# Moving one more of the four token blocks of each product by B from ScalarE to GpSimd in a fused selective-scan and mixture-of-experts kernel

## The reference, cut to what matters

```python
def _mamba_block(x, p):
    xn = _rmsnorm(x, p['norm_w'])
    xz = xn @ p['Win']
    xp, z = jnp.split(xz, 2, axis=-1)
    xc = jax.nn.silu(_causal_depthwise_conv(xp, p['conv_w'], p['conv_b']))
    dbc = xc @ p['Wx']
    dt, Bm, Cm = jnp.split(dbc, [DT_RANK, DT_RANK + D_STATE], axis=-1)
    delta = jax.nn.softplus(dt @ p['Wdt'] + p['bdt'])
    A = -jnp.exp(p['A_log'])
    y = _selective_scan(xc, delta, A, Bm, Cm, p['Dp'])
    y = y * jax.nn.silu(z)
    return x + y @ p['Wblk']
```

## Time and profile before

| | |
|---|---|
| median of 3 runs | 2395.76 us (2388.49 to 2397.93) |
| the profiled execution | 2392.5 us |
| its span, first to last instruction | 2390.7 us |
| first and last scan begin at | 67.5 and 1929.9 us |
| busy over the whole span | PE 1910.8, DVE 1957.4, ACT 1697.5, POOL 1414.9 us |
| busy in the first 1822.6 us after the first scan (67.5 to 1890.12) | PE 1415.4, DVE 1572.5, ACT 1488.2, POOL 1359.8 us |
| mean granted clock of TensorE | 0.934 |

### The profile page before, as it was taken

The page is one execution under the profiler, slowest core; times in us unless marked ns, Lnnn a source line. Parts: engine busy times, 40 slices in busy tenths (PEclk is TensorE's granted clock), DMA queues, the critical chain, the costliest instruction groups (busy, mean ns, idle before and its releaser), DMA issues. The chain is left out here.

```text
span 2390.7 us, 35098 instructions
## 1 busy us (share of the span) xinstructions
PE 1910.8 (80%) x10784; PEld 1200.9 (50%) x10784; DVE 1957.4 (82%) x1824; ACT 1697.5 (71%) x3050; POOL 1414.9 (59%) x1365
## 2 busy tenths in 40 slices
PE   5677777777777777777777777777778669999998
PEld 2344444444444444444444444444444348998998
DVE  3688888888888888888888888888888977776775
ACT  3787888788878888888888888888878723333333
POOL 2477777777777777777777777777777720000000
PEclk8789999999999999999999999999998879999999
DMA  7222222222222222222222222222222400000000
GB/s 225 70 57 70 59 73 59 68 56 73 58 73 57 70 55 70 55 70 55 70 55 70 56 70 58 72 58 72 58 69 58 127 1 10 10 10 10 9 5 10
DMA packets 81482, 139.49 MB, mean 58 GB/s; under 512 B 21264, under 2 KB 39312, under 8 KB 76816
## 3 DMA queue, kind: packets, MB, share of 16 engines
q1 hardware_dynamic: 75024, 120.36, 19.5%
q10 hardware_dynamic: 6400, 18.42, 2.5%
HBM read 63.85 MB, written 7.74 MB: 30 GB/s over the span
## 5 line engine op out<-in xcount | busy, mean ns | idle before, releaser
L801 DVE TENSOR_TENSOR_SCAN scan<-decay,dbu_ps 128x1024 f32<-128x1024 f32 x512 | 1156.7, 2275 | 180.7 <-PE dbu_ps L1017 174.7
L466 POOL TENSOR_TENSOR scan<-scan,c_rep 128x1024 f32<-128x1024 f32 x256 | 748.2, 2923 | 485.9 <-DVE scan L801 418.2
L1017 PE MATMUL dbu_ps<-ident,scan 128*128 128x128 f32 x4096 | 597.5, 295 | 392.2 <-DVE scan L801 274.0
L1017 PEld LDWEIGHTS dbu_ps<-ident,scan 128*128 128x128 f32 x4096 | 500.1, 151 | 711.9 <-DVE scan L801 370.8
L545 ACT ACTIVATE decay<-d_rep,a_cur 128x510 f32<-128x510 f32 x1024 | 676.8, 710 | 138.3 <-DVE scan L801 90.9
L623 ACT ACTIVATE scan<-du_t,b_t 128x256 f32<-128x256 f32 x1024 | 443.0, 495 | 64.0 <-PE dbu_ps L1017 62.8
L460 POOL TENSOR_SCALAR scan<-du_t,b_t 128x256 f32<-128x256 f32 x896 | 473.6, 544 | 0.0
L810 DVE TENSOR_TENSOR scan<-scan,c_rep 128x1024 f32<-128x1024 f32 x256 | 347.0, 1356 | 0.0
L1002 PE MATMUL y_ps<-scan,sel 128*32 128x512 f32 x2048 | 301.4, 663 | 4.9 <-POOL scan L466 4.9
L739 ACT ACTIVATE decay<-dbu_ps 128x512 f32<-128x512 f32 x256 | 148.4, 597 | 207.2 <-PE dbu_ps L1189 195.8
L1029 PE MATMUL pre_ps<-xn,w_pre 128*128 128x512 f32 x512 | 230.7, 603 | 6.0 <-DVE w_pre L790 5.2
(11 more groups left out here) (105 smaller groups left out, 1805.0 us busy)
## 6 DMA issues: line engine op xcount, KB each, us to landing
d_rep<-delta SPq DMA_DIRECT2D x1024, 64.0 KB, 2.0
c_rep<-c_rows SPq DMA_DIRECT2D x32, 1024.0 KB
w_pre<-prepared_weights ACTq DMA_DIRECT2D x15, 866.0 KB, 7.9
prepared_weights<-scan SPq DMA_DIRECT2D x3, 1122.0 KB, 24.0
scan<-in_conv_w SPq DMA_DIRECT2D x4, 512.0 KB, 4.8
w_out<-prepared_weights SPq DMA_DIRECT2D x16, 128.0 KB, 6.2
sp_e<-in_x_rows SPq DMA_DIRECT2D x8, 256.0 KB, 3.2
d_rep<-in_w ACTq DMA_DIRECT2D x2, 1024.0 KB, 7.5
```

The lines of the kernel that those rows point to most:

```text
L466: nc.gpsimd.tensor_tensor(ring[slot % RING], ring[slot % RING], c_rep[par][:, slot // PRS, :].unsqueeze(1).broadcast_to([128, 2, TG]), ALU ...
L801: nc.vector.tensor_tensor_scan(ring[slot % RING].rearrange("p u t -> p (u t)"), decay[slot % DEC].rearrange("p u a t -> p (u a t)"), dbu_p ...
L1017: last = nc.tensor.transpose(dbu_ps[slot % 2][:, u, 128 * j:128 * j + 128], dbu_t[m % 2][:, j, b, :, :].rearrange("p q c -> p (q c)"), ide ...
```

## The change

POOL_J goes from 2 to 3: POOL makes 12 of the 16 instructions of each block, ACT 4. The tables of ACT are scaled to it (1, 2 and 1 per block; 1 and 3 for the first block). POOL's tables count q, so they stay, and each q now has three instructions. Arithmetic, data, buffers and all other instructions are the same.

```diff
-POOL_J = 2
+POOL_J = 3
...
-SHARE = (0, 3, 6, 8)
-FIRST = (0, 3, 8)
+SHARE = (0, 1, 3, 4)
+FIRST = (0, 1, 4)
```

## The result

| | before | after |
|---|---|---|
| median | 2396.85 us (4 runs, 2388.49 to 2398.66) | 2515.41 us (4 runs, 2512.49 to 2517.82) |
| ratio, with its 95% interval | | 1.0501 [1.0474, 1.0529] |
| span of the profiled execution | 2390.7 us | 2514.2 us |
| mean granted clock of TensorE | 0.934 | 0.874 |
| line 832 to line 832, mean of all windows | 58.58 us | 62.46 us |

Slower by 118.6 us. The forecast was 2421, its range 2400 to 2462: the direction is right, the size is missed by 94 us. The difference lies in the windows: 30 x (62.46 - 58.58) = 116 us.

A forecast was written before the change was run, and what follows sets the result against it. No engine was full; a chain through PE, ACT and DVE to line 832 set the window. Profiled 2392.5 + 24.6 for windows + 1.0 for edges = 2418, run 3.3 below median, so 2421 us; range 2400 to 2462.

The forecast's parts named there:

- passes through PE's unbroken run to slot 5 and to `dbc`: Slots 4 to 5: PE's release 1.36 us later carries through unchanged to slot 5 and `dbc`.
- 0.82 was forecast: Whole window: 1.36 - 1.59 + 0.6 + 0.45 = +0.82 us, over 30 windows +24.6.
- Slot 4's slack and release, +1.36: Block 1, slot 4: POOL's 0.46 us slack against 1.82 of new work releases PE 1.36 us later.
- first rival: Block 1's second burst: third POOL instruction loses to DVE's product by C, 0.96 us later; 2450 us, chance 0.24.
- ACT's saving, -1.59: Between the copy of `dbc` and the softplus, eight ACT instructions become four: -1.59 us per window.
- Softplus, +0.6: Block 3's first POOL burst reaches into DVE's softplus at line 832: +0.6 us, bounds 0 and 1.37.
- the second and third would have lost a whole 0.455 each: Softplus: full blocking of the shared ports makes the loss 1.1 instead of 0.6; rival at 2436 us, chance 0.10.
- Slot 10, +0.45: Slot 10: one more POOL instruction ahead of `du` delays `du`, DVE and slot 12 by 0.45 us.
- the release by line 460: Slot 4, sign: PE's wait is released by POOL's line 460 and not by ACT's line 623.
- the sign of the first rival: Slot 4: release later than 2 us, with one line 460 instruction of 1.4 us in the second burst.
- The period of 58.8: Sign: the period of slot 15, one window's length, near 58.8 us.
- the waits in slots 4 and 5 of 2.2 together: Sign: DVE's waits in slots 4 and 5 come to about 2.2 us together.

The follow-up runs named there:

- the clock held in both: Changed kernel with 34, 24 and 10 fillers (idle PE work in slots 4, 11, 12): 2431.29 us; kernel before with 14, 24 and 9: 2377.99 us.
- block 2 alone: Kernel before with only block 2 of each step at 12 POOL instructions, the other blocks at 8: 2377.91 us, 0.9943.
- the filled kernels: Kernels with PE fillers (identity transposes, zero products) that change no result; changed kernel with 34, 24 and 10: 2431.29 us.
- 14, 20 and 7 fillers: Kernel before with only block 2 at 12 POOL instructions, plus PE fillers ahead of slots 4, 11 and 12: 2377.53 us, 0.9944.
- block 0 changed: Kernel before with only block 0 of each step at 12 POOL instructions, the other blocks at 8: 2429.72 us, 1.0143.
- block 3 alone: Kernel before with only block 3 of each step at 12 POOL instructions, the other blocks at 8: 2481.33 us, 1.0365.
- the changed kernel with 16 and with 16 and 24 fillers: Changed kernel plus 16 identity transposes ahead of slot 4's wait: 2483.83 us; with 24 zero products in slot 11 as well: 2487.05 us.
- eleven instructions: Changed kernel with block 1 at 11 POOL and 5 ACT instructions, second burst two long: 2488.01 us; with 22, 24 and 10 fillers: 2383.00 us.

## Why the prediction was wrong, point by point

The gap of 118.6 us in parts, each kernel taken against the kernel before of its own session: 52 us with the clock held in both; 82 us that the changed kernel loses to the lower clock; less 15 us that the kernel before itself loses without fillers. 52 + 82 - 15 = 119.

- **The step that failed** is the sentence that the +1.36 "passes through PE's unbroken run to slot 5 and to `dbc`". It took the run from slot 4 to slot 5 to be 4.36 us long whenever it starts. It is 6.18 to 7.04 us, as TensorE's clock is low at its start. That is +1.8 to +2.7 us at slot 5, and 0.2 to 1.7 us more than forecast behind slot 9 (`du`, slot 12 and slot 15). In the mean of the three windows that repeat, slot 4's release adds 2.42 us, the run to slot 5 2.17, the chain to line 832 -1.60, the softplus 0.32 and the rest 1.25: 4.56 where 0.82 was forecast. The mean clock of 0.934 stood in the table of the time before, and the views of a stretch would have shown where its low part lay and that in most windows nobody waited there. They would also have shown its price: where it did lie between slot 4 and slot 5, that way took 6.06 us instead of 4.36 and the window 1.7 to 2.0 us more. The forecast did not ask what a longer pause, or a low stretch somewhere else, would cost. The Trainium skill's page TensorE: Matmul & The Clock Gate (section Part 1: The HAM clock gate (the "warmup" mystery)) says that the throttled clock is the default and activity releases it; by that rule the longer idle time alone would have raised the question. The trace agrees for 5.37 and 5.57 us of idle time. The run with block 2 alone shows the low clock behind 2.44 us as well. Why the low stretch falls where it does stays open.
- **Slot 4's slack and release, +1.36.** Right: POOL closes slot 4. The first rival came on top with its price: the third instruction lost to DVE, 1.04 us measured, 0.96 worked out, and DVE was first by the few hundredths foreseen. I gave it 0.24 because POOL's instructions follow without a gap; that did not save its turn. That rival's sum was 1.78 per window and 54 us; with the clock held in both, 1.68 and 53 us were measured. Part of that closeness is luck, since slot 4 came 2.52 us later in these two kernels instead of the 2.32 of that sum, and the softplus cost 0.32 instead of 0.6. The mechanism was priced rightly and its chance was too low.
- **ACT's saving, -1.59.** Right: from the copy of `dbc` to line 832 it is 14.50 us instead of 16.10, -1.60, in the filled kernels too.
- **Softplus, +0.6.** The collision is there and half as large: 1.38 instead of 1.23 for two of the three, 0.32 in all. Line 832 itself lost nothing to POOL. As the prediction read the Trainium skill's page SBUF — State Buffer (section SBUF: two separate sides), the second and third would have lost a whole 0.455 each; the rows show 0.15 each, less than the span of a POOL instruction.
- **Slot 10, +0.45.** Right: 2.69 instead of 2.25 us.
- **What would show it.** Several of the named signs came: the release by line 460, 1.4 us before line 832, the product by C at 2.7, ACT's busy time down by 197 us, and the sign of the first rival, a release more than 2 us later with a second burst of 2.42 us. The period of 58.8 and the waits in slots 4 and 5 of 2.2 together did not: they are 61.8 to 63.2 and 2.62 + 2.39. POOL's busy time rose by 327 us and not 230, and line 832 itself stayed at 1.23 us. A reader of these signs would have seen at once that the excess lies between PE's start in slot 4 and in slot 5.

## What to carry to other kernels

Where PE pauses in every round, look up where its clock is low now and who waits there, before moving any release ahead of it: here a release 2.43 us later went with work behind it that took 1.8 to 2.7 us longer. An experiment is only comparable if the clock is the same in both kernels; fillers in PE's pauses make it so, but only if every pause is filled far enough: with part of the filling the low stretch merely moved, and with 14, 20 and 7 fillers it still came on `du`. And count the start times of two engines that share SBUF to the hundredth: a race with 0.03 us between the two is decided the same way in every window, and the loser paid 1.04 of the winner's 1.19 us.

## What the runs showed of the hardware that was not expected

- **The low stretch moves.** With pauses of nearly the same length just ahead, the transposes of slot 4 took 1.09 us in the kernel before (2.54 us) and 1.96 with block 2 changed (2.44 us); with block 0 changed both came behind 2.44 us. What of the rest of the window decides it was not settled. Four kernels with quite different work (block 3 alone, the changed kernel with 16 and with 16 and 24 fillers, eleven instructions) settled into windows of the same length, 61.43 to 61.45 us, and three others (before, block 2 alone, block 2 with fillers) into 58.02 to 58.03. Why is open too, but it means that a term may be right and yet not show in the time: block 2 alone has 1.60 us less on ACT's chain than before and the same window.
- **Matmuls that do nothing can save time.** 68 per window took 84 us off the changed kernel.
- **POOL and DVE at SBUF.** The loss depends on who is first and on what follows: 1.04 us for a POOL instruction of 0.455 behind a DVE product by C of 1.19; 0.15 us for a DVE instruction of 1.23 under a burst of short POOL instructions, where the burst lost the more (eight take 6.57 us at 1037.44, 8 x 0.455 = 3.64 undisturbed); 3.30 us for a DVE product by C behind two POOL products in a row. Which of these ways a meeting goes was not foreseen from the spans alone.
